# TensorE's order inside a block: like-shaped matmuls side by side in an attention and mixture-of-experts kernel

## The reference

```
x = x + attention(layernorm(x))      # linear attention, 16 heads of 16 channels, a decay per head
x = x + experts(layernorm(x))        # 8 experts of width 896, the best two for each token
```

```
att       = r @ k                      # scores inside a chunk
y         = (att * Wmat) @ v + r @ state * wb
new_state = ws * state + (k * wk) @ v
```

## Time and profile before

| | |
|---|---|
| median of 3 runs | 891.09 us (890.43 to 891.14) |
| span of the profiled execution, first to last instruction | 873.5 us |
| median less that span | 17.6 us |
| mean granted clock of TensorE | 0.991 of 2.4 GHz |
| TensorE busy | 838.0 us, 96% |
| VectorE, ScalarE, GpSimd busy | 498.1, 489.4, 467.3 us |
| phase one, TensorE's loop | about 24 to 305 us |

### The profile page before, as it was taken

One profiled execution on the slowest core, in us unless ns is written; L12 is line 12 of the kernel. 1 busy time (PEld: TensorE's weight loads), 2 busy tenths in 40 slices (PEclk: granted clock), 3 DMA queues, 4 the chain that ended last, 5 costly groups with the idle time before them and its releaser, 6 DMA issues. The chain is left out here.

```text
span 873.5 us, 17506 instructions
## 1 busy us (share of the span) xinstructions
PE 838.0 (96%) x6343; PEld 678.9 (78%) x6343; DVE 498.1 (57%) x1237; ACT 489.4 (56%) x876; POOL 467.3 (53%) x497
## 2 busy tenths in 40 slices
PE   3999999999999998999999999999999999999995
PEld 2677777777777776887898788898888888887884
DVE  6788788889888766243443443543443544352441
ACT  4578788788878887254543543533543543452331
POOL 4434777777787666475434455344355352436214
PEclk9999999999999999899999999999999999999998
DMA  5852122112111122654234144333235142404113
GB/s 158 324 201 68 52 96 77 65 57 82 39 39 51 48 79 74 203 153 82 95 68 88 56 106 90 98 67 73 72 95 99 57 104 25 123 3 50 15 17 42
DMA packets 50471, 74.01 MB, mean 85 GB/s; under 512 B 5056, under 2 KB 42176, under 8 KB 50368
## 3 DMA queue, kind: packets, MB, share of 16 engines
q1 hardware_dynamic: 35488, 53.46, 18.4%
q0 software_dynamic: 14592, 19.18, 12.8%
q10 hardware_dynamic: 288, 0.01, 0.0%
HBM read 38.41 MB, written 34.22 MB: 83 GB/s over the span
## 5 line engine op out<-in xcount | busy, mean ns | idle before, releaser
L1568 POOL DMA_INDIRECT out<-ysb,index x80 | 124.6, 1557 | 147.0 <-DVE ysb L1804 110.8
L1917 PE MATMUL p<-xh,whi 128*128 128x512 f32 (+1 forms) x504 | 190.2, 377 | 4.0 <-PEq L1470 4.0
L1781 DVE TENSOR_TENSOR hid<-gated,p 128x512 f32<-128x512 f32 (+1 forms) x126 | 80.9, 642 | 193.2 <-ACT gated L1630 192.9
L1918 PE MATMUL p<-xl,whi 128*128 128x512 f32 (+1 forms) x504 | 189.9, 377 | 0.0
L1919 PE MATMUL p<-xh,wlo 128*128 128x512 f32 (+1 forms) x504 | 189.5, 376 | 0.0
L1630 ACT ACTIVATE gated<-p 128x512 f32<-128x512 f32 (+1 forms) x126 | 70.9, 563 | 174.0 <-PE p L1919 174.0
L1943 PE MATMUL py<-w,hh 128*128 128x512 f32 x448 | 163.3, 405 | 4.0 <-DVE hl L1070 3.3
L1557 POOL TENSOR_TENSOR wlo<-wraw,whi 128x448 fp32r<-128x448 f32 x56 | 71.1, 1273 | 97.2 <-ACT whi L1616 92.4
L1917 PEld LDWEIGHTS p<-xh,whi 128*128 128x128 f32 x504 | 94.7, 188 | 25.3 <-issue 6.6
L1942 PE MATMUL py<-w,hl 128*128 128x256 f32 x384 | 108.9, 284 | 0.2 <-issue 0.2
L1919 PEld LDWEIGHTS p<-xh,wlo 128*128 128x128 f32 x504 | 94.7, 188 | 18.6
(11 more groups left out here) (204 smaller groups left out, 1452.0 us busy)
## 6 DMA issues: line engine op xcount, KB each, us to landing
wraw<-in_w SPq DMA_DIRECT2D x24, 896.0 KB, 4.9
disp<-wraw SPq DMA_DIRECT2D x16, 662.5 KB, 9.1
xtok<-disp SPq DMA_DIRECT2D x16, 530.0 KB, 5.6
x_ring<-in_x SPq DMA_DIRECT2D x16, 256.0 KB, 3.0
out<-x SPq DMA_DIRECT2D x16, 256.0 KB, 2.2
xtok<-disp SPq DMA_DIRECT2D x8, 265.0 KB, 4.0
out<-ysb,index POOLq DMA_INDIRECT x80, 3.8
disp<-row,slot_i POOLq DMA_INDIRECT x64
```

The costliest lines, as they stand in the source:

```text
L1568: nc.gpsimd.indirect_dma_start(out, bass.IndirectOffsetOnAxis(ap=index[e.const % 2][:, t:t + 1], axis=0), ysb[j % NY][:], None, compute_op ...
L1781: nc.vector.tensor_tensor(hid[k][:, 0:w], gated[k][:, 0:w], p3[k][:, 0:w], ALU.mult).then_inc(hid_ready, 1)
L1917: nc.tensor.matmul(dst[:, 0:w], hi[m][:, wcut], xh[xcut], start=(kt == 0), stop=False)
L1918: nc.tensor.matmul(dst[:, 0:w], hi[m][:, wcut], xl[xcut], start=False, stop=False)
```

## The change

Three lines move in TensorE's loop; nothing is added or taken away. scores_b(c) goes behind within(c, 0, 1), within(c, 0, 2) and within(c, 0, 3), so the four value products of the first tile follow each other. project_r(c + 1) and project_k(c + 1) follow each other, with nothing between. within(c, 1, 3) goes ahead of count and turn2, so the four value products of the second tile follow each other too. The epilogue is not changed.

```diff
@@ -1357,19 +1357,19 @@
             project_g(c)
             outer(c)
             within(c, 0, 0)
-            scores_b(c)
             within(c, 0, 1)
             within(c, 0, 2)
+            within(c, 0, 3)
+            scores_b(c)
             project_r(c + 1)
-            within(c, 0, 3)
             project_k(c + 1)
             across(c, 1)
             within(c, 1, 0)
             within(c, 1, 1)
             within(c, 1, 2)
+            within(c, 1, 3)
             count(c - 3)
             turn2(c - 2)
-            within(c, 1, 3)
             project_o(c - 1)
             logits(c - 2)
             turn_k(c + 1)
```

## The result

The changed kernel takes 884.67 us (median of 4 runs, 884.24 to 885.08) against 890.76 us for the kernel before beside it: a ratio of 0.9936, with a 95% interval of 0.9923 to 0.9948. It is 6.1 us faster, where 11.4 us and 879.7 us had been forecast; it lies above the range of 877.5 to 883.0.

The account below looks back on a forecast made before the run. TensorE's instruction stream was taken to bound phase one's blocks; fewer tile-shape switches save 9.48 + 0.79 + 0.455 + 0.65 = 11.4 us, so 891.1 - 11.4 = 879.7 us, range 877.5 to 883.0.

Parts of the forecast that it names:

- from the fourth block on TensorE's instruction stream alone sets the pace: Phase one's loop: blocks repeat every 19.01 us, so a shorter TensorE stream shortens each block, by 0.79 us.
- What lies around the span stays: Outside the profiled span: the median's 17.6 us above it stays, so 891.1 - 11.4 = 879.7 us.
- an engine that waited for anything would vary: Phase one's blocks: their identical 19.01 us lengths were taken to show that TensorE waits for nothing.
- The sum of switches: TensorE's loop: five tile-shape switches fewer save 0.79 us a block, 11.4 us in all.
- The estimate drawn from: TensorE's loop: five switches fewer at some 175 ns per drain would be 0.88 us a block.
- rival 1: Scores straight to a full group is dear: 881.4 us at its bounds' end; slower than before, 2 in 100.
- the middle of the bounds: Scores to project_r: entry costs 0.11 us, between nothing and 0.11 us more; 1.7 us either way over 15 blocks.
- The covers: Other engines' waits in a block: enough slack remains that none holds TensorE, such as 0.77 us before VectorE's masks.
- rival 2: Group sums wait for VectorE's residual (margin 0.14 us): 882.8 us, with lesser losses 882 to 886; 13 in 100.
- 0.65 + 0.455 + 2 x 0.79: First blocks' gains: 0.65 us in block 0, 0.455 in block 1, 0.79 each in block 2 and the next.
- rival 3: Seam to phase two: one slow-clock stretch more or less, 878.3 or 881.1 us; more than that, 7 in 100.
- Rival 4: Phase one: TensorE's stream is not the pace, so no change, 891 us; 3 in 100.

Follow-up runs that it names:

- e5_no_scatter_before: The kernel before without the 64 scatter DMAs, so no routed rows are written: 876.62 us, ratio 0.9844.
- e9_weight_low_late_after: The changed kernel with GpSimd's low weight piece moved from ahead of the mix to the end of its turn: 876.93 us, ratio 0.9852 to before.
- e4_no_scatter_after: The changed kernel without the 64 scatter DMAs, so no routed rows are written: 864.59 us, ratio 0.9706 to before.
- e7_z_first_after: The changed kernel with scaled(c - 1) ahead of normed1(c + 2) on ScalarE: 885.48 us, ratio 0.9941 to before.
- e8_rstd_z_first_after: The changed kernel with group_rstd(c - 1) ahead of turned1(c + 1) and scaled(c - 1) ahead of normed1(c + 2) on ScalarE: 882.17 us.
- e10_weight_low_late_before: The kernel before with GpSimd's low weight piece moved from ahead of the mix to the end of its turn: 887.94 us, ratio 0.9982.
- e11_split_scatter_after: The changed kernel with each block's four scatter DMAs in two pairs, the second tile's behind norm1: 883.84 us, ratio 0.9929 to before.

## Why the prediction was wrong, and where it was right

**The step that failed is "from the fourth block on TensorE's instruction stream alone sets the pace".** On it rests the sum's largest term, 12 x 0.79 = 9.48 us for blocks 3 to 14. In those blocks the order gave 3.9 us (0.80 in the first, 3.1 in the eleven behind it), because from the fifth distance on the pace is set by a loop over the scatter DMAs, turn1's late release, ScalarE and GpSimd: 20.41 us in the block that was read.

**Where the mistake came from** is the step "What lies around the span stays". The prediction took the 17.6 us between the profiled span and the median as time outside the span. Time less span is 2.0 us in both kernels' later profiles; 14.1 of the 17.6 us lie in the loop (295.38 less 281.30), nearly all of it in the blocks in which releases by TensorE come late, and the other 1.5 us before and behind it. The profiled execution happened to be one without late releases, and it looks like e5_no_scatter_before (873.5 and 874.9 us of span; 19.01 us a late block in both). So TensorE's stream set the pace in the execution that was read and not in those that are timed. A gap of 2% between a span and the median of the same program was on the table and should have been a rival: another execution, with another bottleneck. That even blocks showed TensorE's pace, since "an engine that waited for anything would vary", was no proof either: the last seven distances of e9_weight_low_late_after are 19.17 to 19.26 us, and TensorE does wait in it (project_r for VectorE's mix, 5.6 us in 7 times).

**The sum of switches was right.** 0.79 us a block was forecast, 0.80 measured without the disturbance (19.01 less 18.21), and 11.43 against 11.4 us over the loop. That the total fits to the last digit is luck in part: the first distance gave 1.12 us (17.33 to 16.21) where 0.65 was put, and the two blocks of 18.53 us gave 0.32 less each. The Trainium skill's page "TensorEngine Tiling (Array Packing)", section "Tiling Modes", says that a change of tiling mode drains the engine; the trace agrees in so far as the five switches that went gave back 0.80 us. The estimate drawn from the Trainium skill's page "TensorE: Matmul & The Clock Gate", section "Single matmul latency" (0.88 us), was a little high.

**The dear junction (rival 1) fell.** Scores take 1.07 us and project_r behind them 1.83 us, the middle of the bounds.

**The covers held in all but two blocks where nothing is held back.** The 0.14 us of margin at the residual (rival 2) was worked out in block 6, a heavy one, and it wasn't there: in e4_no_scatter_after the group sums come 0.25 us late, for the residual, in two of the three such blocks, and the block takes 18.53 us. The prediction counted the cover to the residual's end, while the group sums start 0.15 us behind it where they wait for it. That cost 0.6 us in all. In the changed kernel itself VectorE is late for the group sums now and then (0.32 us at 188.58, 2.5 us in 5 times from 65 to 310 us), as rival 2 named it. It accounts for no more than half of the missing gain even if all of it counted, and e9_weight_low_late_after gets back more than is missing without a change on VectorE.

**Where the missing gain went.** Of 12.0 us that the order is worth without the scatters, about 6 are left with them. By the starts of project_v the gain is 2.75 us over the first four distances, where the prediction's terms give 0.65 + 0.455 + 2 x 0.79 = 2.7, and only 3.1 us over the eleven behind, where they give 8.7. There the new order runs into the loop of ScalarE, GpSimd and the scatters; the old order was at 20.26 us on average, in the seven last blocks read through the same loop (20.32 to 20.73 us), in the three before them with a wait for across in it. That e7_z_first_after changes nothing, e8_rstd_z_first_after 2.5 us and e9_weight_low_late_after 7.7 us, is what such a loop would do.

**The seam and the clock (rival 3)** are not in it: from the last project_v to phase two it is 48.1, 48.5 and 48.9 us in the three profiled executions, from there to the end 523.3, 524.0 and 523.4 us, with a mean granted clock of 0.991, 0.994 and 0.991. Rival 4 (no change) fell too.

**What stays open.** Why the execution profiled ahead had no late releases, though its scatter DMAs overlap turn1 in much the same way (188.95 to 193.90 us, turn1 at 191.58), isn't known; none of the eight other profiles with four DMAs in a row shows such blocks. What in the DMA issue holds TensorE's releases, and so whether they are really sent late or seen late, isn't shown either: only that it comes with these DMAs, and that turn1's and outer's came behind the last of them. Nor is it known why TensorE's stream breaks inside outer while they go out. That the late blocks of the changed kernel vary between some 19.5 and 20.8 us was not followed up.

## What to carry to other kernels

Put the profiled execution's span beside the timed median before any sum: where they differ by more than usual (1.7 to 2.1 us in every other run here), the trace that is read is of another execution than those that count, and its bottleneck may be another one. An even block length is no proof of which engine sets the pace. A saving in the stream of the busiest engine is worth its full sum only until the next loop closes; look for that loop in the waits of the other engines, and take work out of it too, since here moving one 1.3 us instruction on GpSimd made 884.67 us into 876.93. Where GpSimd issues DMAs one behind the other, look which completions fall due meanwhile: here they were what the loop hung on, and spreading the DMAs only moved the stall.

## What the runs showed of the hardware

- While GpSimd issued indirect DMAs (0.97 to 1.11 us each, four in a row), TensorE's completions reached ScalarE and VectorE late: 2.85 us for a transpose, 1.0 us for scores, in the block shown. The transpose's came 0.83, 0.96 and 0.93 us behind the last DMA's end in the blocks read of after, e9_weight_low_late_after and e10_weight_low_late_before (196.49, 193.01 and 198.72), outer's 0.42 us in e11_split_scatter_after. TensorE broke its stream without a written wait, by 0.29 to 0.47 us at a time. One execution, the one profiled ahead, shows none of this with the same DMAs.
- Leaving the DMAs out took 14.2 us (old order) and 19.1 us (new order) off the span, and leaving out half of them (new order) 19.1 us as well, by the profiled spans.
- Going from 32x128 tiles straight to full ones cost no more than by way of 128x32 tiles: scores 1.07 us and the full group behind them 1.83 us.
